# A selective-scan and mixture-of-experts block: for 51 of 128 scan units, scanning in place in PSUM and taking the product with C in halves straight behind the scan

## What is computed

```python
x_dbl = xc @ x_proj_w.T
dt, Bm, Cm = jnp.split(x_dbl, [DT_RANK, DT_RANK + D_STATE], axis=-1)
delta = jax.nn.softplus(dt @ dt_w.T + dt_b)
A = -jnp.exp(A_log)
dA = jnp.exp(jnp.einsum('bld,dn->bldn', delta, A))
dBu = jnp.einsum('bld,bln,bld->bldn', delta, Bm, xc)

def step(h, inp):
    dA_t, dBu_t, C_t = inp
    h = dA_t * h + dBu_t
    y = jnp.einsum('bdn,bn->bd', h, C_t)
    return (h, y)
```

## Time and profile before

| | us |
|---|---|
| median of 3 executions | 879.68 |
| lowest and highest | 877.77, 882.72 |
| the profiled execution's own time | 878.53 |
| its span | 876.8 |
| DVE busy | 726.0 |
| PE busy | 666.4 |
| POOL busy | 568.7 |
| ACT busy | 508.1 |

### The profile page before, as it was taken

The page is one execution under the profiler, slowest core; times in us unless marked ns, Lnnn a source line. Parts: engine busy times, 40 slices in busy tenths (PEclk is TensorE's granted clock), DMA queues, the critical chain, the costliest instruction groups (busy, mean ns, idle before and its releaser), DMA issues.

```text
span 876.8 us, 13126 instructions
## 1 busy us (share of the span) xinstructions
PE 666.4 (76%) x3706; PEld 487.0 (56%) x3706; DVE 726.0 (83%) x1128; ACT 508.1 (58%) x1092; POOL 568.7 (65%) x488
## 2 busy tenths in 40 slices
PE   4458588778768886798688767878785788898964
PEld 2134455445345545684477446744674467798863
DVE  1388798989998999979999999999999986474363
ACT  2546686866768586547746575557643664433421
POOL 1095475567857896789768985888669945355322
PEclk9778599899979988999899989988897879999997
DMA  6824133223313336533653364434553334457793
GB/s 176 256 98 134 42 123 105 76 72 112 120 49 100 102 111 198 160 112 99 185 158 119 91 188 149 124 107 135 173 147 93 97 100 120 138 159 221 216 317 112
DMA packets 95450, 118.24 MB, mean 135 GB/s; under 512 B 11351, under 2 KB 63395, under 8 KB 95363
## 3 DMA queue, kind: packets, MB, share of 16 engines
q1 hardware_dynamic: 90835, 108.02, 41.8%
q0 software_dynamic: 4544, 9.38, 2.9%
HBM read 105.37 MB, written 16.34 MB: 139 GB/s over the span
## 4 chain that ended last, share of the span: by engine, by line
PE 34%; DVE 32%; issue 14%; ACT 11%; DMA 4%; SPq 3%; POOL 2%; DVEq 0%; ACTq 0%; POOLq 0%
DVE state L964 16%; PE work_front L1120 5%; PE y L1168 4%; DVE product L974 3%; PE y L1164 3%; PE gate L1263 2%; PE up L1281 2%; PE work_front L1126 2%; PE up L1270 2%; ACT decay L828 2%; DVE stats L894 2%; DMA y_dram<-y_rows,x_rows 1%; DVE tanh_c L939 1%; PE work_side L1204 1%; PE y L1157 1%
## 5 line engine op out<-in xcount | busy, mean ns | idle before, releaser
L708 POOL TENSOR_TENSOR inflow<-du,b_wide 128x1024 f32<-128x1024 f32 x128 | 315.1, 2465 | 163.8 <-DVE product L974 101.5
L964 DVE TENSOR_TENSOR_SCAN state<-decay,carry,inflow 128x512 f32<-128x512 f32 x192 | 234.8, 1264 | 6.1 <-ACT decay L828 6.0
L828 ACT ACTIVATE decay<-delta,a_neg 128x512 f32<-128x512 f32 x256 | 172.5, 688 | 105.6 <-DVE state L964 101.5
L974 DVE TENSOR_TENSOR product<-state,c_wide 128x1024 f32<-128x1024 f32 (+1 forms) x98 | 137.4, 1403 | 3.3 <-PE y L1164 2.3
L1164 PE MATMUL y<-ident,product 128*128 128x128 f32 x704 | 110.1, 301 | 36.9 <-DVE product L974 36.8
L735 POOL DMA_INDIRECT y_dram<-y_rows,x_rows x78 | 84.5, 1084 | 79.2 <-ACT y_rows L884 70.6
L1164 PEld LDWEIGHTS y<-ident,product 128*128 128x128 f32 x704 | 90.1, 156 | 74.9 <-DVE product L974 43.5
L1168 PE MATMUL y<-h_rows,ident 128*128 128x512 f32 x160 | 93.6, 679 | 1.2 <-ACT h_rows L793 0.7
L729 POOL DMA_INDIRECT row_dram<-m_tok,place x64 | 71.0, 1110 | 24.6 <-issue 18.4
L964 DVE TENSOR_TENSOR_SCAN state<-decay,inflow 128x512 f32<-128x512 f32 x64 | 74.6, 1207 | 8.4 <-ACT decay L828 5.9
L1120 PE MATMUL work_front<-u_t,w_tap 128*128 128x512 f32 x128 | 66.3, 647 | 6.0 <-ACT u_t L763 4.4
(11 more groups left out here) (210 smaller groups left out, 1318.8 us busy)
## 6 DMA issues: line engine op xcount, KB each, us to landing
b_wide<-bc_dram SPq DMA_DIRECT2D x128, 256.0 KB, 3.3
w_stage<-gate_up_dram SPq DMA_DIRECT2D x78, 344.0 KB, 4.1
c_wide<-bc_dram SPq DMA_DIRECT2D x98, 256.0 KB, 3.5
x_rows<-row_dram SPq DMA_DIRECT2D x78, 65.0 KB, 3.3
x_tok<-in_x SPq DMA_DIRECT2D x8, 256.0 KB, 6.4
out<-x_tok SPq DMA_DIRECT2D x8, 256.0 KB, 4.8
inflow<-y_dram SPq DMA_DIRECT2D x6, 256.0 KB, 4.5
gate_up_dram<-in_Wg SPq DMA_DIRECT2D x1, 1376.0 KB, 8.9
```

The source lines that it names most:

```text
L708: e.tensor_tensor(inflow[:, key % 3], du[:, c % 2], b_wide[:, key % ROW_SLOTS:key % ROW_SLOTS + 1, :].to_broadcast([P, HALVES, CHUNK]), AL ...
L828: e.activation(decay_bank[h][:], delta[:, c % 2, h, :], ACT.Exp, scale=a_neg[:, h, n:n + 1]).then_inc(S["decay"], 1)
L964: e.tensor_tensor_scan(state[:, key % STATE_SLOTS, h, :], decay_bank[h][:], inflow[:, key % 3, h, :], 0.0 if c % (SEQ // CHUNK) == 0 else ...
L974: e.tensor_tensor(product[:, key % 2, :, :wide], state[:, key % STATE_SLOTS, :, :wide], c_wide[:, key % ROW_SLOTS:key % ROW_SLOTS + 1, :wi ...
```

## The change

In *in-place* units, `scan` writes the states over the decays in `decay_bank[h]`, and `times_c` is put straight behind the scan: two instructions of 128 x 512, each reading states from PSUM and `c_wide` from SBUF. The decays of the next unit now come from a step `carry_decay` on ACT: for each half it waits for that half's product, copies the last column from the bank to `carry` (128 x 1), waits for that copy, and then writes the decays into the bank. `inflow` of three units later waits for the scan alone.

In-place units are those with an expert tile (33), and n = 0, 3, 8, 9 of the other chunks' units behind chunk 0 that have no share (18): 51 in all. Semaphores `times_c` and `carry` now count halves.

```diff
+IN_PLACE = (0, 3, 8, 9)
...
         put("scan", i)
-        fetch("decay", i + 1)
-        put("carry", i)
         moving = ("up", m) in done
+        in_place = moving or i not in shares and c > 0 and n in IN_PLACE
+        if in_place:
+            put("times_c", i)
+            put("carry_decay", i + 1)
+        else:
+            fetch("decay", i + 1)
+            put("carry", i)
...
-        put("times_c", i)
+        if not in_place:
+            put("times_c", i)
...
                     if key >= 3:
-                        if share[key - 3] < SUB:
+                        if key - 3 in in_place or share[key - 3] == SUB:
+                            e.wait_ge(S["scan"], HALVES * (key - 2))
+                        else:
                             e.wait_ge(S["times_c"], products[key - 3])
...
-                        if key:
+                        if name == "carry_decay":
+                            e.wait_ge(S["times_c"], products[key - 1] - 1 + h)
+                            e.activation(carry[:, UNITS[key - 1][1], h:h + 1], decay_bank[h][:, CHUNK - 1:], ACT.Copy).then_inc(S["carry"], 1)
+                            e.wait_ge(S["carry"], HALVES * (key - 1) + h + 1)
+                        elif key:
                             e.wait_ge(S["scan"], HALVES * (key - 1) + h + 1)
...
-                        e.tensor_tensor_scan(state[:, key % STATE_SLOTS, h, :], decay_bank[h][:], inflow[:, key % 3, h, :],
+                        e.tensor_tensor_scan(decay_bank[h][:] if key in in_place else state[:, key % STATE_SLOTS, h, :], decay_bank[h][:], inflow[:, key % 3, h, :],
...
+                    if key in in_place:
+                        for h in range(HALVES):
+                            e.wait_ge(S["scan"], HALVES * key + h + 1)
+                            e.tensor_tensor(product[:, key % 2, h, :], decay_bank[h][:], c_wide[:, key % ROW_SLOTS, :], ALU.mult).then_inc(S["times_c"], 1)
```

30 lines of the change are left out of this document (16 added, 14 removed).

## The result

The changed kernel takes 891.5 us (median of 4 runs, 889.0 to 897.3) where the kernel before, timed beside it, takes 880.2 (877.8 to 882.7): 1.2% slower, ratio 1.0121 with a 95% interval of 1.0085 to 1.0157. Its profiled execution took 888.99 us, 887.2 of them span.

What follows compares the result with a forecast made beforehand. DVE, busy 83% of the span, was taken to bound the kernel. Terms 1.2 + 0 + 8.5 - 2.4 - 2.4 - 4 + 1 = +1.9 on 878.53 gave 880.4; with 1.15 for the median, 881.6 us, range 870 to 892.

Steps and rivals of the forecast that it cites:

- Product halves +1.2: In 51 in-place units, two product halves from PSUM cost 0.03 us more than one whole product: +1.2 us.
- scan into PSUM 0: 102 scan instructions writing to PSUM cost nothing extra: 0, with bounds of -5.8 to +5.8 us.
- rival (b): In-place instructions are dearer, scans by 0.057 us and halves by 0.03: 8.9 us in all, so 890 us; chance 0.17.
- estimate of +6.6 us for reading PSUM: A higher fixed cost for PSUM input, 0.065 us for each of 102 product halves: +6.6 us, speaking against the change.
- Decays later, +8.5: Decays wait for product halves; from n = 8 to 10, where ACT's list is full, this is not hidden: +8.5 us.
- The sign named as the surest: DVE waiting 1.5 to 2 us for decays ahead of the scan of n = 10 in chunks 1 to 6.
- Waits that the product fills, -2.4: Mainly at n = 3, the product is already done where DVE waited for another engine: about -2.4 us.
- Chunk 7, n = 2, -2.4: The product there, 3.58 us long with a wait inside, would take 1.2: -2.4 us.
- Waits inside instructions that go, -4: Mostly n = 4 to 6: POOL's inflow starts sooner, so DVE's instructions are held less; -4 us, bounds -20 and +6.
- New waits inside instructions, +1, bounds 0 to +10: Inflow, starting at the scan's end, runs over other work at n = 8, 9, 12 and 14: +1 us, bounds 0 and +10.
- Rival (a): POOL's waits dissolve (-15 instead of -6.4 us), or scans into PSUM reach their lower bound: 872.6 us; chance 0.26.
- rival (c): ACT's stretch grows further through held silu_g and residual add, and late decays at n = 0 to 3: +5.6, 887 us; chance 0.17.

Runs made afterwards that it cites:

- e8: Kernel before, with the product's wait for the scan moved behind its waits for the row of C and PE: 887.6 us against 877.8, ratio 1.0104.
- e12: Changed kernel, all 51 units in place, with the scan's wait first and whole products adding 1 to their semaphore, not 2: 886.8 us against 885.6, ratio 1.0027.

## Why the prediction came out as it did

The forecast was 881.6 us, +0.2%; the result is 891.5, +1.2%, half a us inside the upper end of the range. The prediction gave the slower side 0.35 and no change 0.40. That the range held is luck as much as insight: some 15 us of gains and as much of losses are missing in the sum. Term by term:

- **Product halves +1.2, scan into PSUM 0.** Right. 0.675 us each, and 1.274 against 1.264 is +0.010, 1 us in all. With that rival (b) falls: it needed 1.30 and 0.68. The estimate of +6.6 us for reading PSUM, which stood beside this term, did not come either; it is three quarters of rival (b)'s 8.9, not the half that the prediction says.
- **Decays later, +8.5.** Right, in mechanism and size. From the end of the scans of n = 8 to the scan of n = 10 I had 11.10 us; chunk 1 has 168.78 - 157.87 = 10.91, and n = 8 and 9 of chunks 1 to 6 grew by 8.0. The runs without n = 8 and without n = 9 show that it is unit 8. In chunks 5 and 6 the late start at n = 7 alone makes the stretch as long (e8), so there the two causes lie over each other. The sign named as the surest, a DVE wait of 1.5 to 2 us ahead of n = 10, was the wrong sign: only chunk 3 has it (1.94 us); elsewhere holds and `x_two`'s wait for PE fill the same time. The length of the stretch was the thing to look at.
- **Waits that the product fills, -2.4** (its parts add up to -2.5). Not there. n = 3 of chunks 1 to 6 came to +0.4 instead: -1.1 in chunk 1, 0 in chunk 4, +1.1 in chunk 6. `x_two` of chunk 4 kept its wait of 1.18 us, where I had PE half a us in hand; why was not tested.
- **Chunk 7, n = 2, -2.4.** Right: -2.3.
- **Waits inside instructions that go, -4.** The mechanism was right and the size too small. n = 4 to 6 of chunks 1 to 6 gained 10.3, and n = 2, which I had not looked at, 8.8. The run with POOL held back gives 13 of these 19 back, so these at least are POOL's head start.
- **New waits inside instructions, +1, bounds 0 to +10.** This is a step that failed. I asked which instructions stand directly behind an in-place scan within 1.2 us, and so found `silu_g`, `du` and a tenth for `choice`. But POOL is a queue. At n = 10 an `inflow` that starts sooner also pulls forward the small operations behind it, and the next `inflow`, a unit later, lands where those had lain: `tanh_c` got +7.3. At n = 14 the `inflow` that the scan releases has small operations and an indirect DMA ahead of it, and so comes 2.5 us behind the scan's end, onto the whole of `choice`: +9.2, where I had 0.1 a unit. The runs without n = 9 and without n = 14 show each.
- **A term that was missing.** The sum had nothing for the order of the three waits ahead of a whole product, nor for the step of 2 on its semaphore, though both stand in the diff. 0.1 us for each of 47 products makes at most the +0.1 at n = 1, 3 and 7 that the units do show. But at n = 7 of chunks 5 and 6 it decides which of two engines goes first. The order alone costs 1.0% in the kernel before; order and step put right take the change from 1.0121 to 1.0027, close to the forecast of +0.2%. That closeness is partly luck: some 16 us of holds that I had not foreseen meet 15 us of gains that I had not foreseen either. Nor is it the only step that would do: n = 9 left out takes off as much.

Rival (a) was half right (the head start is good for at least 13 us) and rival (c) half (holds grow, though not where it put them).

What stays open: n = 3 of chunk 0 was 5.4 us long in the profiled executions of the kernel before and of two variants, and 7.0 to 8.2 in the others, with nothing in place there; and the part behind the last unit varied by 10 us between profiled executions (that of e12 is the longest, though its median is not). Neither was followed up. The change also gives ACT's copy to `carry` a step of 2, and changes what the scans themselves wait for; e12 leaves both in, and no run has them alone.

## What to carry to other kernels

Where instructions of two engines can hold each other and their queues run in step, look at who starts first, and by how much: a margin of 0.04 us decided over 2.2 us here, so every wait ahead of the instruction counts. Look which wait the instruction carries itself, and let that be the one that ends last (here: written first, and with a step of 1); touch neither order nor step of a semaphore without timing that alone. When an engine's queue gets a head start, follow it to the next two or three entries of that queue, not to the first, and when a change with many sites comes out even or worse, try it by site: 35 of these 51, with the waits and the step as they were, were worth 1.1%.
